# Graph attention layer: normalisation in halves, gate bias by an adding DMA, batch 0's first values by matrix products

## What is computed

```python
h = jnp.einsum('bnd,ade->bane', feat_in, W)
th = jnp.tanh(h)
attn = attn_src + jnp.swapaxes(attn_dst, 2, 3)      # th @ w_src, th @ w_dst, per head
attn = jnp.where(attn >= 0, attn, 0.2 * attn)
attn = softmax(jnp.where(~adj, -999.0, attn), axis=-1)
feat_out = elu(jnp.einsum('banm,bame->bane', attn, h) + b)
gate = sigmoid(feat_in @ H_w.T + H_b)
out = layernorm(x + gate * feat_out + (1.0 - gate) * feat_in)
```

## Time and profile before

| what | us |
|---|---|
| median of 3 runs | 703.05 |
| lowest, highest | 701.02, 703.74 |
| profiled execution, its own time | 703.12 |
| its span in the profile | 701.1 |
| one batch in the loop | about 41.1 |
| busy share of the span: TensorE, VectorE | 95%, 92% |
| busy share: GpSimd, ScalarE | 79%, 61% |

### The profile page before, as it was taken

The page is one execution under the profiler, slowest core; times in us unless marked ns, Lnnn a source line. Parts: engine busy times, 40 slices in busy tenths (PEclk is TensorE's granted clock), DMA queues, the critical chain, the costliest instruction groups (busy, mean ns, idle before and its releaser), DMA issues.

```text
span 701.1 us, 12636 instructions
## 1 busy us (share of the span) xinstructions
PE 665.0 (95%) x3403; PEld 381.7 (54%) x3403; DVE 647.0 (92%) x1148; ACT 430.6 (61%) x935; POOL 555.9 (79%) x430
## 2 busy tenths in 40 slices
PE   8799999999999999999999999999999999999883
PEld 5555655555556565555656555565656556564431
DVE  7599999999999999999999999999999999999796
ACT  5524648485683847668384765839476584946554
POOL 2635797979979797997979799797979979796653
PEclk9999999999999999999999999999999999999997
DMA  5643446465354545545555555455545544454402
GB/s 195 191 118 131 151 124 217 112 193 156 137 194 122 200 129 176 156 149 187 128 181 148 153 173 156 166 136 192 150 140 171 163 172 125 161 151 139 148 31 90
DMA packets 49243, 107.12 MB, mean 153 GB/s; under 512 B 3074, under 2 KB 28420, under 8 KB 49220
## 3 DMA queue, kind: packets, MB, share of 16 engines
q1 hardware_dynamic: 38724, 82.06, 35.2%
q0 software_dynamic: 2304, 12.58, 9.7%
q10 hardware_dynamic: 8192, 12.19, 4.7%
HBM read 93.85 MB, written 12.98 MB: 152 GB/s over the span
## 4 chain that ended last, share of the span: by engine, by line
PE 66%; ACT 17%; issue 7%; POOL 3%; DVE 3%; ACTq 1%; DMA 1%; DVEq 0%; POOLq 0%; SPq 0%
PE out_T L965 33%; PE hg L881 25%; PE tr L973 6%; ACT y L543 4%; ACT att_T L506 3%; ACT xT_hi L445 3%; ACT scratch L530 2%; DVE ew L743 1%; PE hg L948 1%; ACT h_sb L457 1%; ACT th L453 1%; ACTq L546 1%; DMA xT_in<-in_xT 1%; ACT adj L487 1%; DVE att L757 1%
## 5 line engine op out<-in xcount | busy, mean ns | idle before, releaser
L743 DVE SCALAR_TENSOR_TENSOR ew<-v_all,u,adj 128x512 f32<-128x512 f32 x768 | 525.7, 734 | 0.0
L965 PE MATMUL out_T<-ew,vals 128*64 128x512 f32 x1536 | 355.9, 599 | 2.4 <-DVE ew L743 2.4
L965 PEld LDWEIGHTS out_T<-ew,vals 128*64 128x64 f32 x1536 | 104.3, 136 | 189.5 <-issue 143.8
L294 POOL TENSOR_TENSOR th_w<-th,score_w 128x768 f32<-128x768 f32 x58 | 127.9, 2206 | 31.3 <-ACT th L453 17.0
L506 ACT ACTIVATE att_T<-out_T,out_bias 128x512 f32<-128x512 f32 x96 | 66.0, 687 | 126.3 <-PE out_T L965 115.3
L881 PE MATMUL hg<-w_hi,xT_hi 128*128 128x384 f32 x384 | 99.6, 368 | 3.1 <-ACT xT_hi L445 1.9
L881 PE MATMUL hg<-w_lo,xT_hi 128*128 128x384 f32 x384 | 89.4, 341 | 0.0
L881 PE MATMUL hg<-w_hi,xT_lo 128*128 128x384 f32 x384 | 88.1, 337 | 0.0
L881 PEld LDWEIGHTS hg<-w_hi,xT_hi 128*128 128x128 f32 x384 | 62.1, 192 | 41.3 <-issue 38.9
L463 ACT ACTIVATE gate_tanh<-hg 128x384 f32<-128x384 f32 x64 | 31.3, 491 | 75.8 <-PE hg L881 75.8
L973 PE MATMUL tr<-ident,att_T 128*128 128x128 f32 x384 | 60.7, 281 | 16.9 <-ACT att_T L506 15.1
(11 more groups left out here) (104 smaller groups left out, 713.0 us busy)
## 6 DMA issues: line engine op xcount, KB each, us to landing
v_all<-v_rows SPq DMA_DIRECT2D x96, 512.0 KB, 3.8
xT_in<-in_xT SPq DMA_DIRECT2D x16, 768.0 KB, 5.0
h_sb<-in_bias POOLq DMA_DIRECT2D x16, 768.0 KB, 6.4
x_in<-in_x SPq DMA_DIRECT2D x15, 768.0 KB, 4.5
out<-y ACTq DMA_DIRECT2D x15, 768.0 KB, 3.5
adj_in<-in_adjT SPq DMA_DIRECT2D x16, 256.0 KB, 5.1
xT_in<-in_x SPq DMA_DIRECT2D x1, 768.0 KB, 6.5
ew<-in_W SPq DMA_DIRECT2D x1, 576.0 KB, 4.1
```

The costliest lines, as they stand in the source:

```text
L294: g.tensor_tensor(th_w[:, c % 2], th[:, c].unsqueeze(1).broadcast_to([P, 2, D]), score_w[:], ALU.mult).then_inc(S["thw_done"], 1)
L743: ve.scalar_tensor_tensor(out=ew[:, (2 * C * j + i) % SLOTS, :], in0=v_all[:, j % VSLOTS, k], scalar=u[:, q, c, h:h + 1], in1=ADJ[c][:], o ...
L965: te.matmul(OUT[VW * k:VW * k + VW, :], vals[:, q, c, h, :], ew[:, t % SLOTS, :], start=(c == 0), stop=(c == C - 1)).then_inc(S["ew_free"], 1)
```

## The change

1. **Gate bias.** The tenth product of `gates` is left out in batches 0 to 14. ScalarE's `gates` now copies the sum out of PSUM (Copy for Tanh), GpSimd issues a second adding DMA per batch (`add_gate_bias`, 768 KB onto `gate_tanh`) after `split_low(b + 2)` and ahead of `variance`, and `gate_quarter` of the next step waits for it and does a Tanh over 1536 columns ahead of its own instruction. Batch 15 keeps the product.
2. **ScalarE's order.** `normalise(b-2)` is two instructions ahead of `copy_out(0)` and two after features 2, with the store's DMA then. `gate_quarter` stands behind `copy_out(1)`, no longer ahead of it.
3. **VectorE's order.** `elu` moves from the end of pair 0 to behind the first `ew` of pair 1; `head_sums(b+1, 0)` one place later; `rden` and `att` one place later in pairs 1 and 5.
4. **Opening.** b is added to batch 0's `h_sb` by four VectorE instructions, which also make the row sums; `v` of heads 0 and 1 is spread by eight products (`spread_first`) and two copies; `gate_low` and the score products of batch 1 move in among pairs 0 and 1; TensorE does attend 0 ahead of the features of batch 1; two more `warm_up` first, six fewer later.

```diff
@@ SyncE, opening @@
+                sp.sem_inc(S["ld_v0"], 16)
+                sp.dma_start(bias_row[:], bias[0:1, :].broadcast_to([P, E])).then_inc(S["ld_b"], 16)
-                for j in range(VSLOTS):
+                for j in range(1, VSLOTS):
                     load_v(0, 0, j)
@@ GpSimd @@
-                pool.wait_ge(S["hcopy_done"], C)
-                add_bias(0)
+            def add_gate_bias(b):
+                pool.dma_start(gate_tanh[:].rearrange("p c d -> p (c d)"), gate_bias_rows,
+                               accum_op=ALU.add).then_inc(S["add_gate_bias"], 16)
                 if ahead:
                     for c in range(C):
+                        if c == 0:
+                            pool.wait_ge(S["gate_done"], C * b + C)
                         split_low(b + 2, q, c)
+                else:
+                    pool.wait_ge(S["gate_done"], C * b + C)
+                add_gate_bias(b)
                 if not first:
                     variance(b - 1)
@@ ScalarE @@
+                    act.wait_ge(S["add_gate_bias"], 16 * b + 16)
+                    a.activation(gate_tanh[:], gate_tanh[:], ACT.Tanh, scale=0.5).then_inc(S["tanh_done"], 1)
                 features(b + 1, 1)
                 if not isinstance(b, int) or b > 1:
-                    normalise(b - 2)
-                copy_out(b, q, 0)
+                    normalise(b - 2, 0, 2)
+                if not first:
+                    copy_out(b, q, 0)
                 features(b + 1, 2)
+                if not isinstance(b, int) or b > 1:
+                    normalise(b - 2, 2, C)
                 features(b + 1, 3)
                 if not first:
                     x_forms(b - 1)
+                copy_out(b, q, 1)
+                if not first:
                     gate_quarter(b - 1)
-                copy_out(b, q, 1)
@@ VectorE @@
+                    ve.tensor_tensor(o, o, bias_row[:].unsqueeze(1).broadcast_to([P, H, E]), ALU.add).then_inc(S["bias_first"], 1)
-                        at = 7 if j in (3, 4) else 5
+                        at = (None, 6, 5, 7, 7, 6)[j]
@@ TensorE @@
-                warm_up(WARM)
+                warm_up(WARM + 2)
-                products((G_BANK_LAST if last else G_BANK)[c], q, c, D, [(gate_bias_sel[:], gate_bias[:])], waits).then_inc(S["g_done"], 1)
+                products((G_BANK_LAST if last else G_BANK)[c], q, c, D, extra, waits).then_inc(S["g_done"], 1)
+            def spread_first():
+
+                for k in range(2):
+                    for c in range(C):
+                        last = te.matmul(V_FIRST[k][:, c * P:(c + 1) * P], v[:, c, k:k + 1].broadcast_to([P, P]), ident[:],
+                                         start=True, stop=True)
```

More of the change, by code:

```diff
@@ L495, in out_biases @@
                     rows = slice(VW * (r % 2), VW * (r % 2) + E)
-                    a.activation(m[rows, :, r // 2], mean_ps[E * r:E * r + E, :], ACT.Copy).then_inc(S["out_bias_done"], 1)
+                    means = mean_first_ps if isinstance(b, int) and b == 0 else mean_ps
+                    a.activation(m[rows, :, r // 2], means[E * r:E * r + E, :], ACT.Copy).then_inc(S["out_bias_done"], 1)
             def copy_out(b, q, j):
@@ L551, in step @@
                     return
+                if first:
+                    copy_out(b, q, 0)
                 features(b + 1, 0)
@@ L739, in edges @@
                         dve.wait_ge(S["adj_done"], C * b + c + 1)
-                    if i == 0:
+                    spread = isinstance(b, int) and b == 0 and j == 0
+                    if spread and c == 0:
+                        dve.wait_ge(S["spread_copied"], k + 1)
+                    if i == 0 and not spread:
                         dve.wait_ge(ld_v[j % VSLOTS], 16 * (2 * b + j // VSLOTS + 1))
@@ L771, in step @@
                     between = {}
+                    if j == 1 and not first:
+                        between[1] = [lambda: elu(b - 1, 1 - q)]
                     if j == 1 and not last:
[L773 removed]
+                        between[3] = [lambda: head_sums(b + 1, 0)]
                         between[8] = [lambda: head_sums(b + 1, 1)]
+                    if j == 0 and first:
+                        between[8] = [gate_low]
                     if j == 1 and first:
[L776 to L779 removed]
+                        between[3] = [lambda: head_products(1, 0), lambda: head_sums(1, 0)]
+                        between[8] = [lambda: head_products(1, 1), lambda: head_sums(1, 1)]
                     if j == 2 and not last:
@@ L919, in gates @@
                     pe.wait_ge(S["w_hi_done"], 2)
-                    waits = {KD: (S["w_lo_done"], 2), 3 * KD: (S["gate_bias_done"], 1)}
+                    waits = {KD: (S["w_lo_done"], 2)}
+                extra = [(gate_bias_sel[:], gate_bias[:])] if last else []
+                if last and c == 0:
+                    pe.wait_ge(S["gate_bias_done"], 1)
                 if c > 1:
@@ L1003, in step @@
                     return
-                if not last:
+                if first:
+                    attend(b, q, 0)
                     features(b + 1, 1 - q, 0)
-                if not first:
+                    features(b + 1, 1 - q, 1)
+                else:
+                    features(b + 1, 1 - q, 0)
                     transpose_out(b - 1, HP - 1)
-                if not last:
                     features(b + 1, 1 - q, 1)
-                attend(b, q, 0)
-                if not last:
-                    features(b + 1, 1 - q, 2)
+                    attend(b, q, 0)
+                features(b + 1, 1 - q, 2)
                 transpose_out(b, 0)
```

89 lines of the change are left out of this document (56 added, 33 removed).

## The result

| | before | after |
|---|---|---|
| median, lowest to highest, us | 703.39, 701.02 to 703.82 (4 runs) | 681.09, 680.92 to 681.88 (4 runs) |
| profiled execution: its time, its span | 703.12, 701.1 | 681.0, 679.2 |
| busy share: TensorE, VectorE, GpSimd, ScalarE | 95, 92, 79, 61% | 96, 95, 83, 67% |

The ratio is 0.9692, 95% interval 0.9668 to 0.9715: 3.1% faster. The forecast was 684.1 us in a range of 679 to 692, so the direction and the range held, and the value was 3 us too high. Four of its terms were mis-sized, in both directions.

What follows compares the result with a forecast made beforehand. TensorE was taken to bound the kernel, with VectorE 1.3 us a batch below it. From 703.12 us, -10.2 - 9.8 + 1.4 - 1.6 - 0.3 + 1.5 = -19.0 gave 684.1 us, range 679 to 692.

Steps and rivals of the forecast that it cites:

- Tenth product: TensorE's gates, batches 0 to 14: sixty products removed at 0.17 us each, -10.2 us.
- three covers: In the loop, GpSimd's DMA issue (0.92 us), the transfer's landing (6.4 us) and ScalarE's tanh (1.57 us) cost nothing.
- Halves: Normalisation split around copy_out 0: the wait at transpose_out 0 goes, 0.75 us in each of 13 steps, -9.8 us.
- Loss by close streams: In the loop, TensorE and VectorE, so close, lose something to each other: 0.1 us a batch, +1.4 us.
- Rival 1: VectorE becomes the bound: elu, later, is held up by weigh, up to 1.8 us a batch; 699, likelier 691; chance 0.17.
- Opening: Before the loop: first ew at 26.5 for 31.79, saving 1.6 us (0 to 3.4); warm-up products save another 0.3.
- the clock: Opening: two more zero products shorten TensorE's pause at the lower clock level, saving 0.3 us, between 0 and 1.1.
- strict turns: Opening: if VectorE and GpSimd alternate, the additions last until about 27.9 and the first ew starts then.
- The lower end, 24.9: Opening: earliest start of the first ew, with spread v ready at about 24.9 and additions done by 24.1.
- Last batch: ScalarE's tanh has no cover there and is added whole ahead of transpose_out 0: +1.5 us, wait 3.6 for 2.11.
- rival 4: Second adding DMA lands late, beyond some 17 us, and ScalarE stops ahead of the tanh; at 19 us about 712; chance 0.02.

Runs made afterwards that it cites:

- e1: Changed kernel with the bias product back in every batch, without the second adding DMA and the tanh of 1536 columns: 689.3 us.
- e2: Changed kernel with the normalisation in one piece again, ahead of copy_out 0: 693.37 us.
- e3: Changed kernel with VectorE's order as before (elu, head sums and rden at their old places): 682.99 us.
- e7: Changed kernel with elu one ew later, behind the second ew of pair 1: 686.28 us.
- e5: Changed kernel with twelve zero products at the start for fourteen: 682.66 us.
- e6: Changed kernel with GpSimd waiting in the opening for VectorE's additions before it makes values or splits x: 679.15 us.
- e10: Changed kernel with eleven zero products in TensorE's pause ahead of the row means in the opening: 681.35 us.
- e4: Changed kernel with copy_out 0 and the first gate chunk ahead of x_forms and normalise in the last batch: 675.89 us.

## Why the prediction was right, and where it was off

**Tenth product: right.** -10.2 forecast; e1 gives 9.75 for 56 and, at 0.174 each, 10.4 for sixty. To take the price from the chain (1.76 against 1.59 for a chunk) and not from the mean of 337 ns was the step that mattered; the mean would have given 20 us. Its three covers held: GpSimd's wait (1.7 left, "near 1" forecast), the landing (9.0 us after issue, not 6.4, against some 17 us of room), and ScalarE's tanh in the loop, 1.48 us from 320.64 on, with `gate` done at 323.8 and its reader on GpSimd at 325.96.

**Halves: right in mechanism, mis-sized.** 0.75 each was taken between 0.65 and 0.90; e2 gives 0.88, 11.4 us for 9.8. The wait alone was too low an end, because the transposes behind a wait take 0.66 for 0.44. The two windows of the earlier trace rows had the whole price in them. A difference of two whole batches is the better row when an engine's wait also changes the work behind it.

**Loss by close streams: not there.** +1.4 forecast, about 0 measured. The two parts of the loop sum to -9.75 - 11.43 = -21.2 by e1 and e2, and the loop gave -21.49. With 0.8 us of slack left VectorE's unevenness still costs TensorE nothing, and e3 shows that even the old places would have done. The slack is a little more than the 0.7 forecast although the batch is shorter (39.55 to 39.63 us for 39.7 to 39.9): VectorE's work is 38.79 us for 39.07, and elu's median went from 2.17 to 1.94. There was no row for this term; it was a caution.

**Rival 1: did not come, and was too dear.** elu starts 0.27 us ahead of weigh, by the margin of tenths that the prediction named. e7 shows that 0.67 us more would have cost 4.4 us in the loop. The rival's "1.8 us more work" is about a whole weigh (1.84), more than the worst that came: elu took 3.36 us at its longest in e7 and 1.75 at its shortest, and paid 0.92 on average.

**Opening: inside its range, mis-sized.** -1.6 for the order and -0.3 for the clock were forecast, -2.6 came, if the four bias products gave 0.7 of the -3.27 there (no run separates them: e1, with a fall of the clock as long as e7's, is only 0.24 behind e7). Counted from the first product it is -2.9, of which the two zero products are 1.3 by e5, above the 1.1 that was their upper end; about 1.6 remain for the order, as forecast. That is a remainder: no run undid the order alone. The additions take 6.4 us; with `s_rel` earlier than thought (19.57) the first `ew` is at 26.07 for 26.5, and not at the 27.9 of strict turns. The lower end, 24.9, was too late: e6 starts at 23.08, with the additions undisturbed and `s_rel` 1.0 us earlier than in the earlier trace rows, and `v` was not the later of the two.

**Last batch: the step that failed.** The wait of 3.6 for 2.11 was forecast to the tenth (3.64), and its price of 1.5 was not: 2.86 came, because the longer pause took TensorE's clock down for the transposes and the products behind them. The prediction had a row of such a fall, after an idle time of 1.90 us, and used it in the opening alone. The sum had no term for a fall behind the pause that grows to 3.6 us, nor the range. The row alone could not have settled it, since the 2.11 us in the same place before had no fall behind them, but it was reason enough for an upper end.

Sum of the corrections: -0.2 for the product, -1.6 for the halves, -1.7 for the loss and the remainder of the loop, -0.7 in the opening, +1.3 at the end: -2.9, and 684.1 - 2.9 = 681.2, against 681.0 for the profiled execution. That it comes out is no further evidence, since the terms are the differences of the three stretches. What is evidence is that e1 and e2, each undone alone, give back the loop but for 0.3 us.

## What to carry to other kernels

Price a wait by the difference of two whole periods, one with it and one without, beside the idle time itself; the work behind a wait may run slower too. Where a change lengthens a pause of TensorE, even off the loop, look at the granted clock behind the pauses of like length, and give a possible fall a term of its own. Two engines that hold each other up are a matter of who starts first, so a place in an order is to be read together with the start of the other engine's instruction, in tenths of a us, and the slack of the engine that pays is taken off the price.

## What the runs showed of the hardware

**The clock after a pause.** TensorE's granted clock fell to 0.50 after pauses of 1.95 us (before, opening), 2.40 (e5, opening), 2.84 or 2.85 (changed kernel, e1, e2, e3, e5 and e7, ahead of the row means) and 3.64 to 3.67 (last batch of the changed kernel, e2, e3, e5, e6, e7 and e10). It stayed at 1.00 after 0.45 to 1.77 (nine kernels, opening), 2.11 (before, last batch), 2.14 (e1, last batch), and after 2.85 in e4, whose opening is that of the changed kernel:

```profile
26.00:28.00 2.00, 2.00 (x10) 1.00 0.83 315
28.00:30.00 2.00, 2.00 (x8) 1.00 0.52 113
```

So the length of a pause alone does not say whether the clock falls, nor how long it stays low behind it. What decides was not found. It makes up to 1.1 us of difference between kernels that are alike there, and the start of the first product another 0.5; that much of a comparison of two of these kernels is not to be read as the effect of an edit, and the three stretches and the count from the first product keep it apart.

**DMAs beside a second adding DMA.** Issues, KB each, median us to landing: the page of the changed kernel.

```profile
xT_in<-in_xT SPq DMA_DIRECT2D x16, 768.0 KB, 8.8
...
gate_tanh<-in_H_b POOLq DMA_DIRECT2D x15, 768.0 KB, 9.0
...
adj_in<-in_adjT SPq DMA_DIRECT2D x16, 256.0 KB, 9.0
```

The new transfer takes 9.0 us where its twin takes 6.3, and two of SyncE's went from 5.0 and 5.1 us to 8.8 and 9.0. They are slower beside the second adding DMA, not by the shorter batch: e1, without it, has 5.4 us for both, and e2, with it and a batch as long as e1's, 8.2 and 8.5. All had room here: no transfer stands in the chains of the loop above. A run with the transfer made longer was not tried, so the point from which rival 4 would decide stays as argued.
